# Graph network on one Trainium2 core: in layer 2 the last group of a pass is turned before two others are turned back

## The reference

```python
def _L2_gnn_ref(x, edge_index):
    K = 16
    ALPHA = 0.1
    loop = jnp.arange(N, dtype=edge_index.dtype)
    row = jnp.concatenate([edge_index[0], loop])
    col = jnp.concatenate([edge_index[1], loop])
    deg = jax.ops.segment_sum(jnp.ones_like(col, dtype=x.dtype), col, num_segments=N)
    deg_inv_sqrt = jnp.where(deg > 0, jax.lax.rsqrt(jnp.maximum(deg, 1e-30)), 0.0)
    norm = (deg_inv_sqrt[row] * deg_inv_sqrt[col])[:, None]
    h = x
    for _ in range(K):
        h_neighbors = jax.ops.segment_sum(norm * h[row], col, num_segments=N)
        h = (1.0 - ALPHA) * h_neighbors + ALPHA * x
    return h
```

## Time and profile before

| | us |
|---|---|
| runs of the kernel before, median (lowest, highest) | 8946.5 (8943.17, 8952.78) |
| span of the profiled execution, first to last instruction | 8950.4 |
| POOL busy in the span | 6658.3 (74%) |
| PE busy | 5474.2 (61%) |
| DVE busy | 4879.1 (55%) |
| layer 2, its first pass's first gather to its last pass's last one | some 4057 to 8113 |

### The profile page before, as it was taken

How to read it: one execution, slowest core, us unless ns; L and a number is a source line. 1 busy time by engine, 2 the same in 40 slices (tenths; PEclk the granted TensorE clock), 3 DMA queues, 4 the chain that set the end, 5 groups by cost and what they waited for, 6 DMA issues and landing times. The chain is left out here.

```text
span 8950.4 us, 111450 instructions
## 1 busy us (share of the span) xinstructions
PE 5474.2 (61%) x23642; PEld 4375.0 (49%) x23642; DVE 4879.1 (55%) x12173; ACT 1977.2 (22%) x5359; POOL 6658.3 (74%) x7008
## 2 busy tenths in 40 slices
PE   7566644444454443346777777877666667766643
PEld 6465533333333332225666666655555556555543
DVE  7687555555555556755555555544444444465444
ACT  2355631111111110633111111100000000056433
POOL 6677677777777777677777777777777777777777
PEclk9777755555555555557777777776777767665555
DMA  7664544444444443434444444443333334333311
GB/s 145 133 178 124 95 108 106 107 105 106 110 113 108 106 102 97 138 72 103 112 112 113 114 115 114 119 104 98 99 98 97 99 97 103 94 98 88 83 45 37
DMA packets 905581, 939.53 MB, mean 105 GB/s; under 512 B 380578, under 2 KB 796456, under 8 KB 904806
## 3 DMA queue, kind: packets, MB, share of 16 engines
q1 hardware_dynamic: 652430, 588.73, 22.0%
q0 software_dynamic: 223680, 320.10, 18.9%
q10 hardware_dynamic: 28794, 23.58, 0.9%
HBM read 560.22 MB, written 399.35 MB: 107 GB/s over the span
## 5 line engine op out<-in xcount | busy, mean ns | idle before, releaser
L1924 POOL DMA_INDIRECT l_g<-tab,l x2898 | 2737.2, 945 | 895.3 <-issue 830.4
L2129 DVE TENSOR_TENSOR_SCAN l_w<-l_m,l_w,bank 96x512 f32<-96x512 bf16 x1248 | 1591.9, 1276 | 2707.3 <-PE bank L1956 2690.3
L1956 PE MATMUL bank<-ident,l_g 128*96 128x128 f32 x5030 | 1171.1, 377 | 1887.8 <-DMA l_g<-tab,l 919.3
L1924 POOL DMA_INDIRECT l_g<-tab,XM x1740 | 1651.0, 949 | 530.7 <-issue 481.4
L1956 PEld LDWEIGHTS bank<-ident,l_g 128*96 128x96 f32 x5030 | 756.2, 172 | 2339.4 <-DMA l_g<-tab,l 1035.7
L1976 PEld LDWEIGHTS bank<-ident,l_w 96*128 96x128 f32 x6272 | 1602.7, 328 | 324.8 <-issue 252.4
L1976 PE MATMUL bank<-ident,l_w 96*128 96x96 f32 x6272 | 1507.1, 401 | 6.8 <-DVE l_w L2129 6.4
L1967 PE MATMUL bank<-XM,ident 128*128 128x384 f32 x1568 | 921.1, 681 | 0.0
L2046 ACT ACTIVATE T<-T,dinv_e 128x96 f32<-128x96 f32 x196 | 57.0, 361 | 1968.2 <-DVE T L2154 1966.2
L419 ACT ACTIVATE tail_y<-bank,tail_of,tail_sc 125x96 f32<-125x96 f32 (+1 forms) x596 | 208.7, 431 | 1236.1 <-DVE tail_of L410 1229.5
L308 PE MATMUL bank<-tail_xt,v 96*96 96x500 f32 (+1 forms) x298 | 275.3, 1025 | 316.0 <-ACT tail_xt L303 316.0
(11 more groups left out here) (330 smaller groups left out, 9739.4 us busy)
## 6 DMA issues: line engine op xcount, KB each, us to landing
tab<-T SPq DMA_DIRECT2D x784, 192.0 KB
row_buffer<-tab ACTq DMA_DIRECT2D x5808, 0.4 KB
tab<-l_o SPq DMA_DIRECT2D x441, 192.0 KB
l_m<-mask_d SPq DMA_DIRECT2D x784, 96.0 KB
l_m<-mask_s SPq DMA_DIRECT2D x490, 96.0 KB
l_g<-tab,l POOLq DMA_INDIRECT x2898
row_buffer<-tab SPq DMA_DIRECT2D x2640, 0.4 KB
l_g<-tab,XM POOLq DMA_INDIRECT x1740
```

The lines of the kernel that those rows point to most:

```text
L1924: nc.gpsimd.indirect_dma_start(out=tile(G[q % RG], t), out_offset=None, in_=tables[0:table_at + (2 - p % 2) * TR, :] if p else first, in_o ...
L1956: last = nc.tensor.transpose(a_bank(q)[0:D, u:GE:U], rows[:, u * D:(u + 1) * D], self.ident[:, :])
L2129: v.tensor_tensor_scan(out=W[q % RW][:, :], data0=masks[q % RM][:, :], data1=a_bank(q)[0:D, :], initial=W[(q - 1) % RW][:, GE - 1:GE] if q ...
```

## The change

In layer 2 every group is turned back in step n + 2, the last two too, which gives a pass 51 steps. So step 48 turns back group 46 alone and then turns group 48; 47 and 48 are turned back in steps 49 and 50, behind it. The product with the own rows is taken out of `turn_back` and is issued one step earlier, just ahead of the turn in its step; in steps 48 and 49 it stands behind the turn. VectorE's and SP's loops get the 51st step, and so does the background work's count of steps.

```diff
@@ -222,7 +222,7 @@
-        return 1 + K1 * (NGP + 1) + len(self.own_steps) + slot // SLOTS * (NGP + 1) + slot % SLOTS + 2
+        return 1 + K1 * (NGP + 1) + len(self.own_steps) + slot // SLOTS * (NGP + 2) + slot % SLOTS + 2
@@ -1713,7 +1713,7 @@
-        steps_of = NGP + (5 if conv else 1)
+        steps_of = NGP + (5 if conv else 2 if smooth else 1)
@@ -1722,7 +1722,7 @@
         def back_at(g):
-            return g + 2 if g + 2 < NGP else g + 1
+            return g + 2 if smooth or g + 2 < NGP else g + 1
@@ -1968,8 +1968,6 @@
                 def turn_back(q):
-                    if smooth:
-                        add_own(q)
                     pe.wait_ge(scanned.sem, scanned.at + q + 1)
@@ -2021,9 +2019,14 @@
+                        own_ahead = smooth and 1 <= g <= NGP
+                        if own_ahead and g < NGP - 1:
+                            add_own(p * NGP + g - 1)
                         if g < NGP:
                             last = turn(p * NGP + g)
                         last.then_inc(stepped.sem, 1)
+                        if own_ahead and g >= NGP - 1:
+                            add_own(p * NGP + g - 1)
@@ -2133,7 +2136,7 @@
-                    if back_at(g) == NGP:
+                    if back_at(g) >= NGP:
                         step_back(dve, q)
@@ -2280,7 +2283,7 @@
-                        for g in range(NGP + 1):
+                        for g in range(steps_of):
@@ -2358,7 +2361,7 @@
-                    for g in range(NGP + (1 if p < final else 8 + late)):
+                    for g in range(steps_of if p < final else NGP + 8 + late):
```

## The result

| | before | changed |
|---|---|---|
| median of 20 runs each, us | 8949.25 (8941.14 to 8956.44) | 8958.58 (8949.32 to 8974.58) |
| ratio to before | 1 | 1.0014, 95% interval 1.0007 to 1.0020 |
| span of the profiled execution, us | 8950.4 | 8953.0 |
| idle ahead of the 2898 gathers of passes 1 to 15, us | 895.3 | 904.3 |

The change makes the kernel slower by about 0.1%, 9 us between the medians. That is inside the 0.2% that I counted as no change, though the interval does not hold 1. The forecast was 8954.5 in a range of 8942 to 8965.

What follows compares the result with a forecast made beforehand. POOL's gathers bound layer 2, with other engines on the path only at seams between passes. Eight waiting seams add 6.1 us and two covered ones 2.0, so +8 gives a median of 8954.5, range 8942 to 8965.

Steps and rivals of the forecast that it cites:

- The seam is what counts, and 11.4 us is all there is to win: Between layer 2 passes, POOL waits for the last group's store; removing these waits could save at most 11.4 us, 0.13%.
- The turn of 48 starts when 48 lands: At a pass's end, 2.49 us behind the end of issue: 1.55 gained in waiting seams, 0.36 lost in covered ones.
- What was ahead of the turn is now behind it, 7.77 to the last scaling: On PE behind the turn of 48: 6.41 plus 1.36 makes 7.77 us to the last scaling, before 5.46.
- Together, 0.76 in each of the eight and 1.0 in each of the two: End of issue to last scaling: 0.76 us later in eight seams, 6.1; 1.0 added in two covered ones; sum +8.
- The eight waiting seams: Of ten seams with the short lot of POOL's writes, the eight where POOL waits; 9.50 us becomes 10.26.
- the two covered ones: Seams into passes 5 and 8, without a wait: 1.67 us later, less 0.65 of cover, 1.0 each.
- The product one step earlier costs nothing: In all other steps, 784 products issued ahead of a turn instead of behind it, costed at nothing.
- The rule on the clock: The skill's rule that waits for data bring the array back to half rate; by it every seam is slow.
- The rival of the low clock in every seam: PE's sequence takes 7.04 us in every seam: +17 us, 8963.5; chance 0.2.
- the quick rate rules: PE's sequence at the seam runs at the quick rate, 5.23 us: -1.4 us, 8945; chance 0.2.
- the turn alone sets the end: At the seam the early turn of 48 keeps its 1.55 us gain, taking all 11.4: 8935; chance 0.05.
- The loop slower than the gathers: TensorE's loop stays above 4.99 us a group in every step; each 0.1 over costs 78 us, 9025; chance 0.02.

Runs made afterwards that it cites:

- e4: The changed kernel with the products of 47 and 48 both ahead of the turn of 48; 8943.5 us, ratio 0.9998 to before.
- e11: e4 run once more for a second trace; 8946.48 us, ratio 0.9992 to before.
- e9: The unchanged kernel before, run once more for a second trace; 8952.39 us, ratio 1.0001 to before.
- e1: The kernel before with only the product one step earlier, 46 and 47 still turned back ahead of the turn of 48; 8951.39 us, ratio 1.0001.
- e2: The changed kernel with the product directly ahead of its turning back as before, so only the 51-step order changed; 8961.77 us, ratio 1.0013 to before.
- e6: The changed kernel without the lots (finished rows POOL writes out between passes) and their loads; 8943.06 us.
- e7: e4 without the lots (finished rows POOL writes out between passes) and their loads; 8911.99 us.
- e8: As e2, but the products of 47 and 48 stand ahead of the turn of 48; 8961.72 us, ratio 0.9991 to before.
- e5: The kernel before without the lots (finished rows POOL writes out between passes) and their loads; 8919.35 us.

## Why the prediction was right

**The seam is what counts, and 11.4 us is all there is to win.** Right. The order e4 takes 10.0 of them (8.4 in its second pair, e11 against e9), and no kernel tried took more. Inside the passes nothing moved: the changed kernel's gathers were busy 2737.6 us and before 2737.2, and the 9.0 us of added idle are the growth of the ten waits.

**The turn of 48 starts when 48 lands.** Right in nine of the ten, with a wait that names the gather, 1.7 to 2.5 us behind the end of issue; at the end of pass 0, where ScalarE first scales the gathered rows, it started 1.2 later than the landing, at 3.25. The mean is 2.22 against the 2.49 that I had from the releases of group 47.

**What was ahead of the turn is now behind it, 7.77 to the last scaling.** Right: 7.45 to 8.44 in the fifteen seams, mean 7.86 in the ten short ones. Reading the length of the new chain off the stretch between the turns of 47 and 48, where the same pieces already stood behind a wait, gave it within 0.1. e4 shows the cause: with the two products out of that chain it is 5.62.

**Together, 0.76 in each of the eight and 1.0 in each of the two.** The sum of 8 held (9.0 in the traces' first pair, 10.3 in the second), its parts less so. The eight waiting seams lost 4.7 us together, not 6.1, mainly since the turn of 48 came 2.27 behind the end of issue and not 2.49; the two covered ones lost 2.28 and 2.09, not 1.0 each. The step that failed is the one that took 5.23 for the sequence in the covered seams "and as much in the other covered one": it read a property of the seam where there was only the clock of that moment. After the change those two seams took 8.44 and 7.65 from turn to scaling, like any other, and their cover was 0.48 and 0.34 where I took 0.65. The second trace of the kernel before says the same: there the seam into pass 8 takes 7.04 for the sequence, and 5.22 stands in the one into pass 7. Two errors of 1.4 and 2.4 went against each other, so it is in part luck that the sum came as near as it did. Of the 4.1 us between the forecast 8954.5 and 8958.58, 2.75 are the base: I had 8946.5 from three runs, and twenty gave 8949.25.

**The product one step earlier costs nothing.** It was not nothing: alone it saves 6.1 us of waiting (e1), since it takes the product of 46 out of the stretch between the turns of 47 and 48. I had the product under PE's wait in every ordinary step, and did not follow it to the seam. Beside the order of the change it hardly shows, 904.3 against 904.6 in e2, where the stretch ahead of the turn of 48 has a wait anyway.

**The rule on the clock.** The rival of the low clock in every seam would have given +17. The seams lie between: 7.45 to 8.44, five of fifteen at the slow rate to the end, the others slow only in part, as in pass 1 above, where the first product takes 1.49 and the second 0.85. In the first trace of the changed kernel 12 of the 15 turns of 48 behind their wait run at the slow rate (1.09 us) and three at the quick one (0.64), behind waits of 2.39 to 2.51 where the slow ones had 1.34 to 2.61; in e2 nine are slow and six quick. So a wait of this kind does not bring the low clock each time, and its length alone does not tell which level follows.

The section "HAM oscillation" of the Trainium skill's "TensorE: Matmul & The Clock Gate" tells of a kernel whose waits for data were longer than these and brought the low rate in each round. The traces here agree with it in direction and not in every seam, and my sentence "by it every seam would be a slow one" took it further than its own case goes.

**The other rivals.** That the quick rate rules, or that the turn alone sets the end, did not happen. The loop slower than the gathers did not either, even at a clock of 0.55: POOL's busy time in a stretch of 256 us is 193.49 before and 193.48 after.

## What to carry to other kernels

Moving the step that starts the critical chain ahead of other work helps only if that work doesn't also have to be done before the chain ends on the same in-order engine: count what the engine has left from the last arrival to the last result, in both orders. Independent preparation (here the products with the own rows) belongs into the wait ahead of the arrival, not behind it (e4 against the changed kernel: 19.0 us less idle). To price a new order, look for a place in the old trace where the same pieces already stand in that sequence behind the same kind of wait, and take its whole spread, clock included, for every place.

## What was not expected of the hardware

The granted clock inside a pass went from some 0.7 to 0.55 with the same instructions in another place. With the product ahead of its turning back, PE's work on a group is one spell behind each landing; with the product ahead of the turn, it is the same work in an order in which part of it is done before the landing. PE's busy time in 256 us rose from 177.10 to 197.26 us with the change, and to 199.95 in e1, where the product's place alone is changed. Why the clock is lower in that order stays open. It moved no time here, as the gathers set the pace.

A gather takes 944 to 945 ns on the mean in ten of the traces and 947 in three (e6, e7 and e8, all on the second chip; e5, on that chip too, has 944). Passes are then 241.2 us long on the mean, from the first gather to the end of the last one's issue, instead of 240.7. At 2898 gathers that makes the 7 us by which the busy time of the 2898 gathers differs between e5 and e6 above, and it is as large as the effects that were sought; what sets it stays open. The time up to layer 2, which no kernel here touched, also varied from 4043 to 4074 us.
